# Merged attention on one Trainium2 core: another order for the beginning, for VectorE and for the products with the values

## The reference, cut to what matters

```python
x = x + _L0_ffn_ref(_layernorm(x), ...)                   # 4 expert outputs per token are added here
x = x + _L1_attn_ref(_layernorm(x), A, BC)                # recurrence: h = h * A + x_t; out = h @ BC
x = x + _L1_xattn_ref(ctx, ctx, _layernorm(x), mask, ...) # attention, 16 heads of 16
x = x + _L1_ffn_ref(_layernorm(x), ...)
...
v, k, q = ... @ Wv.T, ... @ Wk.T, ... @ Wq.T
energy = jnp.einsum('nqhd,nkhd->nhqk', q, k)
attention = jax.nn.softmax(energy / jnp.sqrt(jnp.float32(E)), axis=3)
out = jnp.einsum('nhql,nlhd->nqhd', attention, v).reshape(N, q_len, H * D) @ Wo.T + bo
```

## Time and profile before

| | us |
|---|---|
| median of 3 runs (range) | 2812.26 (2808.93 to 2823.7) |
| the profiled execution, its own time | 2824.53 |
| its span | 2822.8 |
| stage `mix_heads`: first instruction to first second energy | 1061 to 1168 |
| its eight batches | 1168 to 1784 |

### The profile page before, as it was taken

One profiled execution on the slowest core, in us unless ns is written; L12 is line 12 of the kernel. 1 busy time (PEld: TensorE's weight loads), 2 busy tenths in 40 slices (PEclk: granted clock), 3 DMA queues, 4 the chain that ended last, 5 costly groups with the idle time before them and its releaser, 6 DMA issues. The chain is left out here.

```text
span 2822.8 us, 40193 instructions
## 1 busy us (share of the span) xinstructions
PE 2320.4 (82%) x12094; PEld 1621.0 (57%) x12095; DVE 1255.2 (44%) x2608; ACT 830.4 (29%) x1871; POOL 884.9 (31%) x1110
## 2 busy tenths in 40 slices
PE   4888685455599983578888889699989999999998
PEld 2444573223377772223333333365569999999997
DVE  4444215552144442567767767258712222222222
ACT  1111110111044441255556666322211221221221
POOL 1000000047600007455535311022225445455443
PEclk9999765778699995689999999899999999999999
DMA  8300110063355546444434310220017777777775
GB/s 282 133 0 0 34 41 16 0 247 116 111 156 156 157 146 101 96 104 98 105 96 99 77 60 27 85 97 30 16 59 236 243 255 237 245 253 236 244 254 161
DMA packets 203554, 360.75 MB, mean 128 GB/s; under 512 B 29302, under 2 KB 182367, under 8 KB 195272
## 3 DMA queue, kind: packets, MB, share of 16 engines
q1 hardware_dynamic: 160456, 299.94, 31.1%
q0 software_dynamic: 43008, 59.70, 10.8%
HBM read 261.83 MB, written 97.13 MB: 127 GB/s over the span
## 5 line engine op out<-in xcount | busy, mean ns | idle before, releaser
L2449 PE MATMUL me_hp<-me_xgT,me_w 128*128 128x160 f32 x3072 | 440.7, 301 | 0.6 <-DVE me_xgT L2491 0.6
L2449 PEld LDWEIGHTS me_hp<-me_xgT,me_w 128*128 128x128 f32 x3072 | 425.1, 191 | 1.5 <-DVE me_xgT L2491 0.7
L1256 DVE TENSOR_REDUCE hd_nmax<-hd_wide 128x2 f32<-128x1024 f32 x256 | 307.8, 1219 | 120.1 <-PE hd_wide L1008 119.5
L1190 ACT ACTIVATE hd_prob<-hd_slim 128x512 f32<-128x512 f32 x512 | 276.3, 601 | 202.6 <-PE hd_slim L1019 201.8
L2505 DVE TENSOR_TENSOR me_hid<-me_act_out,me_hp 128x160 f32<-128x160 f32 x384 | 123.4, 321 | 372.0 <-ACT me_act_out L2477 372.0
L2458 PE MATMUL me_op<-me_hid,me_w 128*128 128x160 f32 x1536 | 236.0, 304 | 0.0
L1019 PE MATMUL hd_slim<-hd_q_stack,hd_k_stack 100*128 100x512 bf16 x512 | 199.0, 392 | 38.9 <-ACT hd_prob L1190 27.5
L1008 PE MATMUL hd_wide<-hd_k_stack,hd_q_stack 97*128 97x512 bf16 x512 | 201.4, 398 | 26.4 <-DVE hd_rest L1251 14.9
L2477 ACT ACTIVATE me_act_out<-me_hp 128x160 f32<-128x160 f32 x384 | 116.4, 303 | 347.6 <-PE me_hp L2449 347.6
L2458 PEld LDWEIGHTS me_op<-me_hid,me_w 128*128 128x128 f32 x1536 | 213.8, 190 | 2.6
L905 POOL DMA_INDIRECT all_x<-outputs,rt_place x128 | 200.6, 1568 | 42.0 <-issue 36.5
(11 more groups left out here) (373 smaller groups left out, 3674.3 us busy)
## 6 DMA issues: line engine op xcount, KB each, us to landing
me_w<-in_L_ffn_w_exp SPq DMA_DIRECT2D x64, 2304.0 KB, 9.0
places<-z_zero SPq DMA_DIRECT2D x23, 1008.0 KB, 11.0
mr_e_xt<-places SPq DMA_DIRECT2D x160, 144.0 KB, 2.2
outputs<-mr_e_y SPq DMA_DIRECT2D x160, 128.0 KB, 1.7
part_rows<-hd_parts SPq DMA_DIRECT2D x48, 256.0 KB, 2.3
hd_k_stack<-part_rows SPq DMA_DIRECT2D x192, 64.0 KB, 2.4
hd_q_stack<-part_rows SPq DMA_DIRECT2D x192, 64.0 KB, 2.7
mr_w<-in_L_ffn_w_in SPq DMA_DIRECT2D x4, 2048.0 KB, 18.3
```

The lines of the kernel that those rows point to most:

```text
L1190: nc.scalar.activation(prob[:, u, :], slim[:, slim_slot(bt, item), :], ACT.Exp, scale=D ** -0.5)\
L1256: nc.vector.tensor_reduce(nmax[:, g % 2, n // 2, c:c + 2], wide[:, at], AX.X, ALU.max, negate=True)\
L2449: last = nc.tensor.matmul(hp[:, f % 3, half * CAP:(half + 1) * CAP], w1[:, sl, c, cols], xgT[:, sl, c, :], start=(c == 0), stop=(c == DC - 1))
```

## The change

1. *Beginning.* Batch 0 and 1 gather their four rows a token into `prob`, which is not used yet, without adding (`gathered_rows`); VectorE adds them (`add_rows`). GpSimd's three small fills go to VectorE. In `BEFORE` the eight first energies of group 0 come ahead of the recurrence of batch 1.
2. *Residue* and part 0 in two halves; the queries' residue moves from step (0, 5) to (0, 7), their second part from (0, 6) to (1, 0), `third_part` from group 0 to group 1. `prep` goes in the order 0, 2, 1, 4, 3.
3. *SP* loads the key pieces as soon as the keys' parts are stored, and the query pieces in two lots.
4. *VectorE*: `turn` ahead of the maxima of step 4; `normed` from ahead of step 0 to step 2; the root (ScalarE) one step later and its reciprocal (`root_of`) in step 1 of the next batch; recurrence items two steps later; `gathered_sums` one step later.
5. *Values*: two key tiles after step 5, two after step 1 of the next group.
6. GpSimd: gathers 5, 5, 6 a group instead of 4, 6, 6; the bias in group 3.

```diff
-        PREP_AT = (0, 1, 2, 4, 6)
-        REST_AT, PART1_AT = (3, 5), (4, 6)
+        PREP_AT = {0: 0, 2: 2, 3: 1, 4: 4, 6: 3}
+        REST_AT, PART1_AT = ((0, 3), (0, 7)), ((0, 4), (1, 0))
...
-        REC_AT = {(1, 3): ("rtp", 2, 0), (1, 5): ("rtp", 2, 1), (1, 7): ("rout", 2, 0), (2, 3): ("rout", 2, 1)}
-        NORM_AT, ADDED_AT = ((1, 0), (1, 2)), ((2, 0), (2, 5))
-        SUMS_AT, CHAIN_AT, ROOT_AT = ((3, 3), (3, 4)), ((3, 5), (3, 6)), (3, 6)
+        REC_AT = {(1, 5): ("rtp", 2, 0), (1, 7): ("rtp", 2, 1), (2, 3): ("rout", 2, 0), (2, 5): ("rout", 2, 1)}
+        NORM_AT, ADDED_AT = ((1, 1), (1, 3)), ((2, 6), (2, 7))
+        SUMS_AT, CHAIN_AT, ROOT_AT = ((3, 4), (3, 5)), ((3, 6), (3, 7)), (3, 7)
...
-            + [("prep", 0, n) for n in (1, 3)] + [("rtp", 1, 0), ("rtp", 1, 1), ("rout", 1, 0), ("rout", 1, 1)]\
-            + [("energy", 0, n // NSTEP, n % NSTEP) for n in range(NSTEP + LEAD)]
+            + [("prep", 0, n) for n in (1, 3)] + [("energy", 0, 0, n) for n in range(NSTEP)]\
+            + [("rtp", 1, 0), ("rtp", 1, 1), ("rout", 1, 0), ("rout", 1, 1)] + [("energy", 0, 1, n) for n in range(LEAD)]
...
-                    sp.wait_ge(stored, (b + 1) * 6 * 16)
+                    for part in range(3):
+                        part_stored(b, 0, part)
+                    sp.wait_ge(stored, b * 96 + 48)
                     for g in range(NG):
-                        stacks(b, g)
+                        stacks(b, g, 0, range(NPAIR))
+                    for part in range(2):
+                        part_stored(b, 1, part)
+                    sp.wait_ge(stored, b * 96 + 80)
+                    stacks(b, 0, 1, range(NPAIR - 1))
+                    part_stored(b, 1, 2)
+                    for g in range(1, NG):
+                        stacks(b, g, 1, range(NPAIR - 1))
+                    sp.wait_ge(stored, b * 96 + 96)
+                    for g in range(NG):
+                        stacks(b, g, 1, range(NPAIR - 1, NPAIR))
...
+                def gathered_rows(r):
+
+                    for j in range(TB):
+                        wait(pool, gathered[j], r * TOP * 16)
+                        for n in range(TOP):
+                            nc.gpsimd.indirect_dma_start(out=row(r, j, n), out_offset=None, in_=outputs[:, :],
+                                                         in_offset=bass.IndirectOffsetOnAxis(ap=place[:, r * TB + j, n:n + 1], axis=0))\
+                                .then_inc(gathered[j], 16)
...
-                        if n == 1 and g > 0:
-                            values(bt.b, bt.slot, g - 1, TB - 1)
-                        if n == 1 and g == 0 and not bt.first:
-                            values(bt.b - 1, 1 - bt.slot, NG - 1, TB - 1)
-                        if n >= 3 and n % 2 == 1:
-                            values(bt.b, bt.slot, g, (n - 3) // 2)
+                        for kc in range(TB // 2):
+                            if n == 1 and g > 0:
+                                values(bt.b, bt.slot, g - 1, TB // 2 + kc)
+                            if n == 1 and g == 0 and not bt.first:
+                                values(bt.b - 1, 1 - bt.slot, NG - 1, TB // 2 + kc)
+                            if n == 5:
+                                values(bt.b, bt.slot, g, kc)
...
+                def add_rows(r):
+
+                    for j in range(TB):
+                        t, at = r * TB + j, (r * TB + j) * TOP
+                        dve.wait_ge(gathered[j], (r + 1) * (16 * TOP))
+                        for n in (0, 2):
+                            nc.vector.tensor_tensor(row(r, j, n), row(r, j, n), row(r, j, n + 1), ALU.add).then_inc(taken, 1)
+                        dve.wait_ge(taken, at + 2)
+                        nc.vector.tensor_tensor(row(r, j, 0), row(r, j, 0), row(r, j, 2), ALU.add).then_inc(taken, 1)
+                        dve.wait_ge(taken, at + 3)
+                        nc.vector.tensor_tensor(x[:, t, :], x[:, t, :], row(r, j, 0), ALU.add).then_inc(taken, 1)
+                        dve.wait_ge(taken, at + 4)
+                        sums(t, 1)
```

More of the change, by code:

```diff
@@ L839, in store_part, with part_stored, stacks @@
                     sp.dma_start(part_rows[a, part].rearrange("(c p) s -> p c s", p=P), parts[:, a, part]).then_inc(stored, 16)
-                def stacks(b, g):
+                def part_stored(b, a, part):
+                    if part == 0:
+                        sp.wait_ge(part0_ready, (b * 2 + a) * DC + DC)
+                    else:
+                        sp.wait_ge((part1_ready, part2_ready)[part - 1], b * 2 + a + 1)
+                    store_part(a, part)
+                def stacks(b, g, a, copies):
                     rows = slice(g * GH * DH, (g + 1) * GH * DH)
[L844 to L847, removed]
+                    stack, which = ((k_stack, K_PARTS), (q_stack, Q_PARTS))[a]
+                    for n in copies:
+                        sp.dma_start(stack[n * DH:(n + 1) * DH, b % 2, g * GH:(g + 1) * GH, :],
+                                     part_rows[a, which[n], rows, :].rearrange("(h e) s -> e h s", e=DH)).then_inc(stacked[g], 16)
                 load_ctx(0)
@@ L1165, in prep @@
                             wait(act, stored, nxt.b * (6 * 16))
[L1166 removed]
+                        for c in range(DC):
+                            nc.scalar.activation(parts[:, n - 2, 0, c, :], wide[:, at, c, :], ACT.Copy).then_inc(part0_ready, 1)
                     else:
@@ L1352, in batch @@
                     r2, r3 = bt.b + 2, bt.b + 3
+                    many = 2 * TB if bt.gathers else TB
                     for g in range(NG):
-                        if g == 0 and nxt is not None:
-                            normed(nxt)
                         for n in range(NSTEP):
+                            if n == TURN_AT and not (bt.first and g == 0):
+                                item = ("turn", 0, g)
+                                turn(bt.b * NG + g, bt.slot if g else 1 - bt.slot, (g - 1) % NG, slim_use(bt, item), slim_slot(bt, item))
                             item = ahead(g, n)
@@ L1359, in batch @@
                                 maxima(item[2], item[3], wide_use(bt, item), wide_slot(bt, item))
-                            if g == 0 and n in REST_AT and nxt is not None:
-                                item = ("prep", 1, REST_AT.index(n) + 2)
-                                residue(nxt.b, REST_AT.index(n), wide_use(bt, item), wide_slot(bt, item))
-                            if n == TURN_AT and not (bt.first and g == 0):
-                                item = ("turn", 0, g)
-                                turn(bt.b * NG + g, bt.slot if g else 1 - bt.slot, (g - 1) % NG, slim_use(bt, item), slim_slot(bt, item))
                             if n == ROWS_AT and not (bt.last and g == NG - 1):
@@ L1368, in batch @@
                                 rows(bt.b * NG + g + 1, (g + 1) % NG, bt.b * (NG // 2) + (g + 1) // 2, slim_use(bt, item), slim_slot(bt, item))
+                            if g == 0 and n == ROOTED_AT and not bt.first and (not bt.static or bt.b + 1 < B):
+                                root_of((bt.b + 1) * TB, 2 * TB if bt.combines else TB, bt.b + 4)
+                            if g == 0 and n == NORMED_AT and nxt is not None:
+                                normed(nxt)
+                            if (g, n) in REST_AT and nxt is not None:
+                                item = ("prep", 1, REST_AT.index((g, n)) + 2)
+                                residue(nxt.b, REST_AT.index((g, n)), wide_use(bt, item), wide_slot(bt, item))
                             if (g, n) in FIN_AT[1:] and not bt.first:
@@ L1416, in _ @@
                     if item == ("rtp", 1, 0):
-                        for pair in range(2):
-                            gathered_sums(1, pair)
+                        add_rows(1)
                         norm_all(TB, TB, 12, 2)
```

78 lines of the change are left out of this document (37 added, 41 removed).

## The result

The changed kernel took 2893.2 us (median of 4 runs, 2884.5 to 2898.5) against 2815.0 (4 runs): ratio 1.0272, 95% interval 1.0234 to 1.0311. I had forecast 2840 with a range up to 2868. The direction was right, the size was not: +78 us instead of +27.5. I call the kernel before the change "before" and the changed one "after". Timelines come from one profiled execution of each; there the span grew by 68.6 us (2822.8 to 2891.4): 13.0 in the beginning and 70.3 in the loop of the stage, less 14.7 outside this stage. The difference timed is the 78 us.

What follows compares the result with a forecast made beforehand. TensorE was taken to bound the loop (68.2 of 79.0 us a batch), a chain the beginning. Beginning +9.5 and loop +18 gave 27.5 over the profiled 2824.5, so 2852; on the median 2840 us, range 2804 to 2868.

Steps and rivals of the forecast that it cites:

- The beginning: Stretch ahead of the first second energy: batch 1's recurrence now stands behind eight maxima, +9.5 us.
- Waits at (0, 3), (0, 5), (1, 0), (1, 5): TensorE's waits in each batch for residues and maxima: costs of +1.6, +2.0, +1.4 and +2.1 us.
- Rival (b): Waits for division, recurrence's norm and bursts vanish in full: -39 us, 2773; chance 0.18.
- Rival (a): The loop comes out even, waits only change places; only the beginning counts: 2822; chance 0.22.
- rival (c): Plain gathers cost 1.57 us or the last copies land after (2, 4): 2858 to 2868; chance 0.10.
- the loop's terms: Costs 7.1 less relief 4.7 give +2.4 us a batch; with the first and last batches, loop +18.
- Bursts in pairs ... -1.4: TensorE's bursts: 0.18 us saved in each of 8 pairs, -1.4 us a batch.
- +1.6: Step (0, 3): no burst there now, TensorE waits 2.4 us for the residue, +1.6 us a batch.
- land at (2, 4), in time: Earlier key pieces and query pieces in two lots land with a microsecond to spare: no cost.
- (3, 5) ... -1.6: Step (3, 5): of the 2.50 us wait for the division, relief of -1.6 us.
- the recurrence's "-1.1": Later recurrence: its norm, read as 2.6 us of waits, is no longer waited for, -1.1 us a batch.
- near +3.0 for the preparation and +3.5 for the division: Per batch: preparation 1.6 and 1.4 us; division 2.0 and 2.1 less 0.6 us.

Runs made afterwards that it cites:

- warm_again: The changed kernel with 37 extra products a batch ahead of five TensorE waits in batches 1 to 6; 2877.9 us, the changed kernel beside it 2888.2.
- add_values: `old_both` plus only the pairs of bursts (two bursts of two key tiles); ratio 1.0071 to the kernel before.
- add_rec: `old_both` plus only the later recurrence, sums, mean, variance and ScalarE's root, and gathers 5, 5, 6; ratio 0.9964 to the kernel before.
- add_prep: `old_both` plus only the preparation's new order, residues and parts, SP's order, later norm and reciprocal; ratio 1.0104 to the kernel before.
- old_both: The changed kernel with the beginning's order and the loop put back; gathered rows and the residue in halves stay; ratio 0.9979 to the kernel before.
- add_turn: `old_both` plus only the division ahead of step 4's maxima; ratio 1.0107 to the kernel before.
- u_turn: The changed kernel with the division behind step 4's maxima again; ratio 1.0256 to the kernel before.

## Why the prediction was wrong

**The beginning: right.** 9.5 forecast, 13.0, 9.9 and 10.7 in the three profiles of the changed kernel (120.1, 117.0 and 117.8 less 107.1), 8 to 12 timed. Maxima of group 0 started 81.8 us after the stage's start, where I had said 79; VectorE's idle time ahead of them and the 8 us of sums behind them are as worked out. The plain gather at 0.96 leaves the rival of dear gathers without ground.

**Waits at (0, 3), (0, 5), (1, 0), (1, 5): right in place and length.** 2.4 to 2.7, 2.0, 2.4 and 2.1 were said, and 2.51, 1.72, 2.30 and 1.72 came. Rival (b) is refuted by its own points of decision: over 1.3 at (0, 3), over 0.5 at (0, 5). The waits that it named did go (`hd_o` 18.6 to 0.9), but others came in their place. Rival (a) too is refuted: the waits did not change places for free. Of rival (c) the dear gathers did not come, the late pieces did, in three batches.

**What failed first: a wait was priced by its length.** The sum had no term for the clock, though the earlier trace rows had shown 0.60 for the one stretch with long waits and 0.98 for the loop. In the loop 30.7 of 70.3 us are TensorE's work at the lower level. That the waits are behind it: with work in five of them `warm_again` runs its loop at 0.96 instead of 0.92, with no busy time left beyond before's and the added products, and takes 10 to 17 us less in spite of 49 us more work; in `add_values` the stretch follows the one wait that grew, in four of six batches. How long a wait must be, and which of several in a row brings the clock down, the runs don't settle: 2.51 us at 1372.01 is followed by full speed, 2.30 at 1387.55 is not. The other half of the excess is idle time, 39.6 us in that loop, where the loop's terms had come to 18.

**"Bursts in pairs ... -1.4": the wrong sign.** In group 2, where nothing is uncovered, a group with pairs takes 17.08 instead of 17.56 us (batch 2 of `add_values` and of before): 0.24 a pair, more than my 0.18. The Trainium skill's rule (*TensorEngine Tiling (Array Packing)*, *Key Properties*: a change of mode drains TensorE) has the same sign; this is all that a trace here shows of it. But a burst is also the work that covers the wait for the residue, and for ScalarE at the batch's end. I counted that at (0, 3) as part of the preparation's move, +1.6, and so missed that the pairs alone uncover it. Measured +26 us.

**A term that the sum lacked, and "land at (2, 4), in time".** The statistics of `gathered_sums` moved one step later with it, and so stand ahead of the first maxima of the next batch. TensorE waits for these 1.7 to 1.85 us at (0, 0) or (0, 1) in six batches of after, and 2.25 to 2.7 at (0, 1) in `add_rec`; the sum had nothing for it. The query pieces were late in three batches (0.46, 2.86 and 1.33 us, 4.6 in all); behind the 2.86 the clock went down, behind the other two it did not. Why `add_prep` waits 13.3 us for exponentials in its loop, `old_both` 7.9 (26.4 less one wait of 18.5 in batch 0), was not looked into.

**"(3, 5) ... -1.6": right in sign and owner; the recurrence's "-1.1": right by luck.** At (3, 5) 1.25 us came off in `add_rec`. The -1.1 was read off wrongly: of the 34.2 us in 8 waits for `hd_xn`, two waits (15.7 and 11.8) lie in the beginning, and the six in the loop are 1.1 each, 6.7 in all. So a batch had 1.1 to win there and not 2.6, and all of it went; rival (b)'s 18.5 for these should have been 6.7. In sum `add_rec` gains 10.5 in the loop's profile and 4 timed.

**Batches, not only waits.** By part the loop's terms were near +3.0 for the preparation and +3.5 for the division in a batch; timed they are 35 / 7 = 5.0 and 36 / 7 = 5.1. Over seven batches I had said 21 and 24.5 us. The loop of `add_prep` is 38.0 longer than that of `old_both`, of which 12.7 are idle time and 25.3 busy time; that of `add_turn` 33.3, of which 20.8 and 12.4. So idle time stayed below what I had said, and the rest is the same products at a lower clock.

What stays open: the four parts and the order sum to 101 us, 12 to 24 more than after lost, which the runs don't resolve; which of several waits brings the clock down; why the exponentials are waited for longer in `add_prep`; and why the first chip was slower in this stage.

## What to carry to other kernels

Where TensorE is the bound at full clock, price each new wait twice: its length, and the work behind it at half clock until it recovers. Several waits of 1.7 to 2.9 us a batch cost here 39.6 us in idle time and 30.7 more in clock. Before moving work to save switching, ask what it covers: a burst worth 1.0 us stood exactly where the residue was late. And run the kernel under study beside every set of its variants, on the same chip: a beginning that was 13 us longer on one chip hid some 20 us of loop.

## What the runs showed of the hardware

A gather of 128 rows that doesn't add holds GpSimd for 0.96 us, one that adds 1.57. Behind waits of TensorE of 2.30 us products of 1.88 us ran in 3.57 (`add_values`) and energies of 0.39 in 0.63 (after), behind one of 2.86 products of 1.99 in 3.76, at a granted clock of 0.51 to 0.54; in the loop of after such stretches last 3 to 7 us, and a wait of 2.51 us had none behind it. With the waits filled (`warm_again`) batches 1 to 6 ran at 0.96 to 1.00. On one of the chips ScalarE stood idle for 21 us in the beginning, released by what the trace calls remote, and in one stretch of `u_turn` there small operations of VectorE that follow one another by a semaphore were 1.24 us apart; the kernel before was 24 us slower there too. Its cause was not looked into.
